# The expert layer of a two-layer decoder: rows of DRAM scattered and gathered by index in place of one-hot matmuls

## The reference, cut to what matters

```python
def _route(tokens, router_w):
    capacity = int(math.ceil(T / E * CAPACITY_FACTOR))     # 2048 / 8 * 1.25 = 320
    probs = jax.nn.softmax(tokens @ router_w.T, axis=-1)
    top1_idx, top1_prob = jnp.argmax(probs, axis=-1), jnp.max(probs, axis=-1)
    order = jnp.lexsort((-top1_prob, top1_idx))
    sorted_e = top1_idx[order]
    counts = jnp.bincount(top1_idx, length=E)
    start = jnp.cumsum(counts) - counts
    keep_sorted = jnp.arange(T) - start[sorted_e] < capacity
    keep = jnp.zeros((T,), bool).at[order].set(keep_sorted)
    return jnp.where(keep, top1_idx, 0)
...
for e in range(E):                                          # E = 8
    h = jax.nn.relu(tokens @ W1[e] + b1[e])                 # 256 -> 1024
    y = h @ W2[e] + b2[e]                                   # 1024 -> 256
    out = out + jnp.where((final_e == e)[:, None], y, 0.0)
x = x + out                                                 # tokens = layernorm(x)
```

## Time and profile before

| | us |
|---|---|
| time, median of 3 runs (6157.39 to 6162.72) | 6161.93 |
| time of the profiled execution | 6163.27 |
| its span | 6161.5 |
| router matmuls start | 5525.35 |
| place counting, first operation to the one behind the loop | 5555.67 to 5685.58 |
| experts 1 to 7, first to last matmul | 5722.80 to 5931.5 |
| last addition to x starts | 6153.33 |

### The profile page before, as it was taken

The page is one execution under the profiler, slowest core; times in us unless marked ns, Lnnn a source line. Parts: engine busy times, 40 slices in busy tenths (PEclk is TensorE's granted clock), DMA queues, the critical chain, the costliest instruction groups (busy, mean ns, idle before and its releaser), DMA issues. The chain is left out here.

```text
span 6161.5 us, 92004 instructions
## 1 busy us (share of the span) xinstructions
PE 5342.2 (87%) x38394; PEld 3103.4 (50%) x38394; DVE 3267.8 (53%) x5810; ACT 2208.3 (36%) x3513; POOL 936.2 (15%) x567
## 2 busy tenths in 40 slices
PE   6799969999999999989998556554499999978999
PEld 3388855666666666654444223222233333335767
DVE  5677744555555545530001678876566666648220
ACT  5634424444444444431111433442144444442100
POOL 0155531110110110000000323423200000000000
PEclk9899989999999999999999788787699999989975
DMA  2311110000000000010000000000000000000200
GB/s 87 129 51 55 46 46 14 9 17 14 9 25 6 9 19 9 6 77 0 0 0 0 25 0 0 0 0 4 24 11 12 1 11 1 1 28 1 82 15 14
DMA packets 34697, 132.00 MB, mean 21 GB/s; under 512 B 6040, under 2 KB 9120, under 8 KB 27568
## 3 DMA queue, kind: packets, MB, share of 16 engines
q1 hardware_dynamic: 34336, 126.75, 5.7%
HBM read 99.48 MB, written 27.26 MB: 21 GB/s over the span
## 5 line engine op out<-in xcount | busy, mean ns | idle before, releaser
L1471 DVE CUSTOM_DVE_ANT_0 ma_prob<-ma_ring,ma_mask 128x400 f32<-128x400 f32 (+1 forms) x1024 | 527.4, 571 | 262.0 <-PE ma_ring L1575 262.0
L1913 DVE TENSOR_REDUCE fa_part<-fa_ring 128x1 f32<-128x512 f32 x768 | 490.0, 685 | 228.8 <-PE fa_ring L2047 157.5
L1869 ACT ACTIVATE fa_prob<-fa_ring 128x512 f32<-128x512 f32 (+1 forms) x832 | 440.8, 600 | 446.6 <-PE fa_ring L2047 363.1
L2027 PE MATMUL fa_ring<-fa_K,fa_Q 32*128 32x512 f32 (+1 forms) x2048 | 538.4, 544 | 2.1
L1484 DVE COPY ma_PT<-ma_ring 128x512 f32<-128x512 f32 x512 | 341.7, 688 | 287.8 <-PE ma_ring L1585 287.3
L2047 PE MATMUL fa_ring<-fa_Qm,fa_K 32*128 32x512 f32 (+1 forms) x1664 | 470.5, 632 | 0.8 <-DVE fa_Qm L1930 0.8
L1585 PE MATMUL ma_ring<-ident,ma_prob 128*128 128x128 f32 (+1 forms) x3328 | 462.2, 280 | 6.7 <-ACT ma_prob L1430 6.7
L1599 PE MATMUL ma_pv<-ma_PT,ma_V 128*64 128x256 f32 (+1 forms) x3328 | 457.8, 393 | 0.0
L2238 PE MATMUL ffn_mid<-ffn_hid,ffn_h 128*128 128x512 f32 x1024 | 441.5, 593 | 9.7 <-DVE ffn_hid L2204 6.3
L1585 PEld LDWEIGHTS ma_ring<-ident,ma_prob 128*128 128x128 f32 (+1 forms) x3328 | 357.1, 141 | 163.6 <-issue 105.1
L2557 DVE TENSOR_TENSOR_SCAN scan_h<-scan_dA,scan_dBx 128x2048 f32<-128x2048 f32 x64 | 407.6, 6369 | 26.4 <-POOL scan_dBx L2431 20.2
(11 more groups left out here) (398 smaller groups left out, 8575.9 us busy)
## 6 DMA issues: line engine op xcount, KB each, us to landing
gd_rows<-gp_tile SPq DMA_DIRECT2D x16, 1024.0 KB, 4.2
gd_c_vg<-gd_rows SPq DMA_DIRECT2D x16, 1024.0 KB
moe_own_w<-in_moe_w SPq DMA_DIRECT2D x14, 1024.0 KB
ma_w<-in_ma_w SPq DMA_DIRECT2D x32, 384.0 KB, 3.2
gd_rows<-gp_gate SPq DMA_DIRECT2D x16, 512.0 KB, 5.1
gd_c_qk<-gd_rows SPq DMA_DIRECT2D x16, 512.0 KB
ffn_h<-in_ffn_h SPq DMA_DIRECT2D x2, 4096.0 KB, 27.1
ma_ctxT<-in_ctxT SPq DMA_DIRECT2D x4, 1601.0 KB
```

The costliest lines, as they stand in the source:

```text
L1471: nc.vector.tensor_tensor_reduce(prob[:, u % 2, t, h, k0:k0 + width], bank("S", u, t, n, h)[:, 0:width], mask[:, b % 2, half * 2 + t, k0:k ...
L1869: nc.scalar.activation(prob[0:n, (u * KT + kt) % PROBS, j, :], bank("scores", u, kt, j)[0:n, :], ACT.Exp, scale=SCALE).then_inc(p_ready, 1)
L1913: ins = nc.vector.tensor_reduce(part[:, t, j, n:n + 1], src[:], AX, ALU.max)
L2027: last = nc.tensor.matmul(bank("chunk", u, i)[:, at * w:(at + 1) * w], Q[rows, b % 2, g, tile * P:(tile + 1) * P], K[rows, b % 2, g, k0:k0 ...
```

## The change

`route`, `own_slots` and `scatter` go, and `experts` becomes one load block, the layernorm, and one block for all the rest.

- The load block stands ahead of the layernorm. SP issues eleven DMAs in it: five small tables, the weights of expert 0, the second biases of all experts (copied to all partitions, 1 MB), the weights of expert 1, and a clearing of the slots in DRAM. The 2 MB table is gone; `before` is 128 x 128.
- Places are counted in three parts: larger ones among the columns from the own tile on, equal and earlier ones within the own 128 columns, larger or equal ones in the columns before. `rival` has two buffers and is computed one tile ahead. After each four tiles six small operations (`seats`) make each token's row number in DRAM: its slot, or a row of its own behind the slots, if it stays with expert 0.
- Expert 0 starts right behind the router matmuls, and the turned rows are made inside its first block. GpSimd (POOL) adds its bias, and its results go to DRAM (`ys`), with no mask.
- POOL scatters the tokens to their slots (`xs`) with one indirect DMA a tile, 16 in all; SP loads each expert's 320 rows; TensorE transposes them (six an expert, two for each tile of slots) and ACT copies them out.
- Experts 1 to 7 run unrolled; DVE adds the bias to the second layer's PSUM, SP stores the 320 rows to `ys`.
- At the end POOL waits for all stores, gathers 16 tiles by index from `ys` with one indirect DMA each, and DVE adds them to `x` in four operations of 128 x 1024.

```diff
-        before = s.sb("before", [P, 2 * B * T])
+        before = s.sb("before", [P, P])
+        with Scope(nc, "moe_load") as first:
+            block = first.block()
+            @block.sync
+            def _(sp):
+                for dst, src in ((router, "router"), (order, "order"), (before, "before"), (token, "token"), (b1, "b1")):
+                    sp.dma_start(dst[:], c.dram[f"moe_{src}"]).then_inc(small_loaded, 16)
+                load_weights(sp, 0)
+                sp.dma_start(b2[:].rearrange("p e d -> p (e d)"), c.dram["moe_b2"].partition_broadcast(P)).then_inc(small_loaded, 16)
+                load_weights(sp, 1)
+                sp.wait_ge(zeros_ready, 1)
+                sp.dma_start(xs[0:SLOTS, :].rearrange("(a p) d -> p a d", p=64), zeros[0:64, :].unsqueeze(1).broadcast_to([64, SLOTS // 64, D])
+                             ).then_inc(cleared, 16)
...
-                chain_t.link(nc.vector.tensor_scalar(hit[:], rival[:], one(mine[:, 1, :], t), 0.0, ALU.is_gt, ALU.add,
-                                                     accum_out=place[:, ds(t, 1), 0]))
-                chain_t.link(nc.vector.scalar_tensor_tensor(out=hit[:], in0=rival[:], scalar=one(mine[:, 1, :], t),
-                                                            in1=before[:, ds(t * -P + B * T, B * T)], op0=ALU.is_equal,
-                                                            op1=ALU.mult, accum_out=place[:, ds(t, 1), 1]))
+                nc.vector.tensor_scalar(hit[:, t * P:B * T], rival[:, t % 2, t * P:], own_prob, 0.0, ALU.is_gt, ALU.add,
+                                        accum_out=place[:, t, 0:1]).then_inc(counted, 1)
+                nc.vector.scalar_tensor_tensor(out=hit[:, B * T:], in0=rival[:, t % 2, t * P:(t + 1) * P], scalar=own_prob, in1=before[:],
+                                               op0=ALU.is_equal, op1=ALU.mult, accum_out=place[:, t, 1:2]).then_inc(counted, 1)
+                if t:
+                    nc.vector.tensor_scalar(hit[:, 0:t * P], rival[:, t % 2, 0:t * P], own_prob, 0.0, ALU.is_ge, ALU.add,
+                                            accum_out=place[:, t, 2:3]).then_inc(counted, 1)
...
+        @block.gpsimd
+        def _(pool):
+            def scatter(g):
+                pool.wait_ge(at_ready, g + 1)
+                for t in range(4 * g, 4 * g + 4):
+                    nc.gpsimd.indirect_dma_start(xs, bass.IndirectOffsetOnAxis(ap=at[:, t:t + 1], axis=0), xn[:, t, :], None
+                                                 ).then_inc(scattered, 16)
...
+            for n in range(2):
+                pool.wait_ge(y0_stored[n], NB // 2 * 16)
+                pool.wait_ge(y_stored[n], len(range(2 - n, NE, 2)) * 32)
+            pool.wait_ge(scattered, NT * 16)
+            for t in range(NT):
+                nc.gpsimd.indirect_dma_start(back[:, t, :], None, ys, bass.IndirectOffsetOnAxis(ap=at[:, t:t + 1], axis=0)
+                                             ).then_inc(back_loaded[t // 4], 16)
...
+            def turn_own(e):
+                pe.wait_ge(taken_loaded[e - 1], 32)
...
+                for d in range(DC):
+                    for j in range(ST):
+                        n = ROWS_OF[j]
+                        last = nc.tensor.transpose(aux[d][:, j * P:j * P + n], taken[0:n, e - 1, j, d * P:(d + 1) * P], c.ident[0:n, 0:n])
+                last.then_inc(own_turned, 1)
...
+                for t in range(4 * i, 4 * i + 4):
+                    if t == NT - 1:
+                        turn_own(1)
+                    second(0, t)
...
+            for e in range(1, NE):
+                pe.wait_ge(w_loaded[e % 2], e // 2 * 32 + 32)
+                pe.wait_ge(own_ready, 2 * e)
+                for m in range(MH):
+                    first(e, None, m)
+                if e + 1 < NE:
+                    turn_own(e + 1)
+                for j in range(ST):
+                    second(e, j)
```

More of the change, by code:

```diff
@@ L3075, in own_slots @@
+        counted = s.sem("counted")
+        seat_steps = s.sem("seat_steps")
+        at_ready = s.sem("at_ready")
+        scattered = s.sem("scattered")
+        taken_loaded = [s.sem(f"taken_loaded{e}") for e in range(1, NE)]
+        own_turned = s.sem("own_turned")
         own_ready = s.sem("own_ready")
@@ L3077, in own_slots @@
         hid_ready = s.sem("hid_ready")
[L3078 to L3090 removed]
+        low_ready = s.sem("low_ready")
+        y0_copied = s.sem("y0_copied")
@@ new lines, in y0_copy, with rows_copy @@
+            def y0_copy(t):
+                act.wait_ge(low_ready, t + 1)
+                if t % 4 == 0 and t >= 8:
+                    act.wait_ge(y0_stored[t // 4 % 2], t // 8 * 16)
+                nc.scalar.activation(y0[:, t // 4 % 2, t % 4, :], low[t % LOWS][:, 0:D], ACT.Copy).then_inc(y0_copied, 1)
+            def rows_copy(g):
+                act.wait_ge(turned, g + 1)
+                for v in range(2):
+                    nc.scalar.activation(row[:, v, g * 512:(g + 1) * 512], aux[v][:], ACT.Copy).then_inc(row_ready, 1)
@@ L3159, in _ @@
-            dve.wait_ge(loaded, 32)
-            for half in range(2):
-                for t in range(HT):
-                    last = nc.vector.tensor_scalar(sits[:, half, t, :], numbers[:], nth[:, 0:1, half * HT + t], None, ALU.is_equal)
-                last.then_inc(sits_ready, 1)
-            dve.wait_ge(xhi_ready, 1)
-            nc.vector.tensor_tensor(xlo[:], xn[:], xhi[:].bitcast(F32), ALU.subtract).then_inc(xlo_ready, 1)
-            by_experts(dve, expert)
+            over = lambda v: v.unsqueeze(2).broadcast_to([P, NT, NE])
@@ new lines, in _, with widen, rivals @@
+            softmax_chain = Chain(dve, softmax)
+            def widen(g):
+                if g >= 2:
+                    dve.wait_ge(turned, g - 1)
+                for v in range(2):
+                    last = nc.vector.tensor_copy(wide[:, g % 2, v], mine[:, v, g * 4:(g + 1) * 4].unsqueeze(2).broadcast_to([P, 4, P]))
+                last.then_inc(wide_ready, 1)
+            done = [0]
+            counts = {}
+            def rivals(t):
+                if t >= 2:
+                    dve.wait_ge(counted, counts[t - 2])
+                nc.vector.scalar_tensor_tensor(out=rival[:, t % 2], in0=row[:, 0, :], scalar=mine[:, 0, t:t + 1], in1=row[:, 1, :],
+                                               op0=ALU.is_equal, op1=ALU.mult).then_inc(rival_ready, 1)
@@ new lines, in _ @@
+            softmax_chain.link(nc.vector.tensor_reduce(mine[:, 0, :], is_top[:], AX, ALU.max))
+            for g in range(GR):
+                widen(g)
+            softmax_chain.link(nc.vector.tensor_scalar(expert_of[:], mine[:, 0, :], -1.0, float(NE), ALU.mult, ALU.add))
+            dve.wait_ge(row_ready, 2 * GR)
+            rivals(0)
+            for t in range(NT):
+                if t + 1 < NT:
+                    rivals(t + 1)
+                count(t)
+                if t % 4 == 3:
+                    seats(t // 4)
@@ new lines, in _ @@
+            pe.wait_ge(small_loaded, SMALL)
+            for t in range(NT):
+                for d in range(DC):
+                    last = nc.tensor.matmul(l_ps[:, t, :], c.xnT[:, d, t * P:(t + 1) * P], router[:, d, :], start=(d == 0), stop=(d == DC - 1))
+            last.then_inc(l_ready, 1)
+            pe.wait_ge(w_loaded[0], 32)
+            for m in range(MH):
+                first(0, 0, m)
+                if m >= 4:
+                    turn_rows(m - 4)
+            for i in range(NB):
+                if i + 1 < NB:
+                    for m in range(2):
+                        first(0, i + 1, m)
+                for t in range(4 * i, 4 * i + 4):
+                    if t == NT - 1:
+                        turn_own(1)
+                    second(0, t)
+                if i + 1 < NB:
+                    for m in range(2, MH):
+                        first(0, i + 1, m)
```

542 lines of the change are left out of this document (208 added, 334 removed).

## The result

The changed kernel took 5843.96 us, median of 4 runs (5842.34 to 5844.57), against 6160.01 of the kernel before (4 runs): ratio 0.9486, 95% interval 0.947 to 0.9503. Forecast were 5855 and a range of 5826 to 5918. The profiled execution has a span of 5842.8 us, 318.7 shorter than before. All of it lies in the expert layer. The list of the page shows the same groups ahead of it, and the last addition of the layer before starts at 5498.70, against 5498.56.

A forecast was written before the change was run, and what follows sets the result against it. Limits taken: layernorm and router, counting beside expert 0, TensorE for seven experts, then 209 us of bringing back at clock 0.50. Following the path through the new block gave span 5853.4 plus 1.8, time 5855; range 5826 to 5918.

The forecast's parts named there:

- Load block: Ahead of the layernorm, which waits for SP's eleven issues: 7.3 us, plus 0.81 for a block start, 8.1 in all.
- To the counting: Router 13.8 us, expert 0's first eight column groups 15.9, four turnings between at 1.5 each; counting starts at 5561.9.
- Counting: VectorE counts places beside expert 0: 91.2 us, ending at 5653.1, where it was 129.9 us before.
- rival B: During counting, POOL's bias additions and DVE exclude each other: counting ends 4.6 us later, time 5860; chance 0.12.
- Hand-over: Expert 0 to expert 1: TensorE waits 7 us for scattered rows, clock loss 2 us; expert 1 starts at 5672.
- C: No wait at expert 1's transposes, 0.33 us an indirect DMA, no half clock: 5831; chance 0.07.
- D: The wait sends TensorE to half clock for experts 1 to 7, up to 144 us more: 5999; chance 0.04.
- Second layers: Experts' second-layer tiles on TensorE: 3.65 us each, three in an expert's 20.8 us.
- The end: Behind the last expert: 16 gathers at 1.3 us, landing 2.2, an addition 1.25; bringing back becomes about 29 us.
- A: Indirect DMAs run one after the other, 20 exposed ones costing 76 us more: 5931; chance 0.12.
- the forecast's own range: Whole time: 5835 (0.5 us an indirect DMA) to 5885 (2.5 us, load block 6 us longer); chance 0.62.

The follow-up runs named there:

- load_beside: Changed kernel with the load block's eleven DMA issues moved into the layernorm's block, beside its work: 5834.8 us.
- rows_early: Changed kernel with the four turnings of the rows behind column groups 1 to 4 of expert 0's first block instead of 4 to 7: 5838.29 us.
- seats_late: Changed kernel with the row numbers of each four tiles (but the last) computed one `rival` operation later: 5841.42 us, one run.
- take_first: Changed kernel with SyncE loading expert 1's slots ahead of the store of expert 0's third group of tiles: 5836.38 us.
- turn_behind: Changed kernel with the transposes of expert 1 behind expert 0's last second-layer tile instead of ahead of it: 5835.37 us.
- all_four: Changed kernel with rows_early, turn_behind, load_beside and the output stored in four pieces, all together: 5824.09 us, ratio 0.9449.

## Why the prediction was right, and where it was off

Its mechanism held, but for one wait that it left out (SyncE's store ahead of the loads, at the hand-over), and the error of 11 us (5855 against 5843.96) is a sum of terms most of which I had put too high. In span times:

| step | forecast | measured | off by |
|---|---|---|---|
| layernorm starts | 5508.2 | 5506.35 | -1.8 |
| router starts | 5524.7 | 5523.20 | -1.5 |
| counting starts | 5561.9 | 5557.28 | -4.6 |
| last seats end | 5653.1 | 5646.1 | -7.0 |
| transposes of expert 1 | 5664.0 | 5657.80 | -6.2 |
| expert 1 starts | 5672 | 5666.59 | -5.4 |
| last second layer ends | 5816.5 | 5807.7 | -8.8 |
| gathers start | 5821.4 | 5811.49 | -9.9 |
| last addition starts | 5844.4 | 5833.45 | -11.0 |
| end of span | 5853.4 | 5842.8 | -10.6 |

**Load block.** Eleven issues at 0.33 to 0.65 us each made 5.5 us, not 7.3 at 0.67. The 0.67 was misread: it spreads the whole way from 9.74 to 16.40 over ten issues, and so holds the meeting and the next block's start, which the sum adds once more as 0.81. The ten issues themselves end at 15.71, 0.60 us each. Their meeting is the layernorm's wait, as load_beside shows. The clearing of the slots landed after 21.2 us and held nobody.

**To the counting.** Some two of the three microseconds here are the four turnings: 1.04 us each, not 1.5. I had taken that from the 32 transposes of the layernorm, which ran at a granted clock of 0.60 (5508.69 to 5514.70 before), where the turnings ran at 1.00 (5547.24 to 5556.06). The order in which they stand costs another 5.2 (rows_early), which the forecast had not asked about.

**Counting.** 91.2 forecast, 88.8 measured, with 3.6 of rival B's lock in it: without POOL's additions 85.1. Of the six microseconds between, four are the 0.25 us of waiting that I had left in each tile: the rows of DVE show none, each operation starts as the one before ends. B's price of 4.6 us for two additions was near. As a case on its own, a time of 5860, it failed, since it added its price to a sum that was too high. Its signs failed as well: I looked for a counting over 96 us and for `rival` well over 2.35 us, and the counting took 88.8 with every `rival` at 2.35; what was held was the short operation of 128 columns. `rival` was held only where seats_late moved the addition onto it.

**Hand-over.** A wait of 7 us was forecast, 7.64 measured, from parts that were off both ways: the scatters at 1.26 us (forecast 1.3), TensorE arriving at 5650.16 instead of 5656.9, and 2.2 us behind SyncE's store that the step had left out (take_first). That the 7 us came out so near is partly luck: the counting was 2.4 us shorter than forecast and TensorE's tiles of expert 0 about 3 us, and the two nearly cancel. The clock fell as forecast and was back for expert 1: six transposes 1.90 us and one tile 5.79, against 1.16 and 3.45 later, 3.1 us for the 2 that I took. C's "no wait" came only with rows_early and turn_behind together, in all_four, and its 0.33 us an indirect DMA did not come at all. D is out: clock 1.00 over experts 1 to 7.

**Second layers.** The mis-sized term: 3.65 us a tile, read where a bias matmul stood between the tiles, is 3.45 without it. Over the 21 tiles of experts 1 to 7, 0.2 us each make 4 us of the time. The same 0.2 us over 15 tiles of expert 0 bring TensorE to the transposes 3 us earlier, but there it waits, so they don't reach the time. Experts are 20.16 us apart (5686.83 to 5706.99) instead of 20.8.

**The end.** Gathers 1.25 us apart (forecast 1.3) and 2.7 to land (2.2). From the last matmul to the last addition's end 27.0 us, "about 29" forecast. A is out: nothing waits for the landing of the one before. The lower bound of the forecast's own range, 5835, is also 4 us off its text: 0.8 us less for each of 20 transfers gives 5839.

By the estimate from the Trainium skill, page DMA: Bandwidth & Descriptors, section on the anatomy of one DMA on the GpSimd path, 20 exposed transfers of 2.3 us one after another would have given 5875. The trace shows a landing of 2.7 us for one gather, but the gathers overlapped, one issued every 1.25 us.

## What to carry to other kernels

Rows that matmuls with a 0/1 table dispatch or bring back can go through DRAM by one indirect DMA for each 128 rows: here 1.25 us each, where 128 tokens had cost 13 us of TensorE at low clock (209 us for 16 tiles). Read what stands in the issuing queue ahead of the transfer that all engines wait for: a store that waited for another engine cost 2.2 us there. After such a rebuild the order of small things is worth looking at again: the transposes that feed the longest chain, the loads in a block of their own and the store in one piece gave 3 to 6 us each by the trace, and with the moved tile of expert 0 17 us of the time together.

## What the runs showed of the hardware

- An indirect DMA of 128 rows of 1 KB holds GpSimd for 0.95 us, the next follows 0.30 later, and it lands after 2.7; with 64 rows it is 0.90.
- The DMA instruction is held while VectorE runs an operation with two SBUF inputs, and ends 0.8 to 1.1 us behind that (2.0 to 3.1 us long in the counting, 1.03 to 1.46 beside the additions). Which part of it is held, fetching the indices or making the descriptors, no run here tells.
- The other way round, GpSimd's addition with two SBUF inputs (2.36 us) holds VectorE's operations with two SBUF inputs: 0.35 us became 1.86, 2.40 and 3.12, and 2.35 became 4.00. Operations with one SBUF input ran beside it at their usual length.
- The low clock after a wait of TensorE is moved, not avoided, by work put ahead of the wait: in turn_behind, behind a wait of 4.27 us, the slow matmuls were expert 1's (10.33 us instead of 8.85). With no wait at all, in all_four, none was slow.
